# Three real products per frequency slot instead of four in the middle phase of a four-layer graph network

## The reference

```
h = relu(bn(conv1d(xc, conv1_w, 0)))        # 1 tap
h = bn(conv1d(h, conv2_w, 8))               # 17 taps, 128 -> 128 channels, padding 8
x_conv = relu(h + xc)
```

## Time and profile before

| | |
|---|---|
| profiled execution, device time | 1127.47 us |
| its span, first to last instruction | 1125.6 us |
| TensorE busy (matmul) | 1072.3 us, 95% |
| VectorE busy | 826.1 us, 73% |
| ScalarE busy | 715.6 us, 64% |
| GpSimd busy | 595.5 us, 53% |
| mean granted TensorE clock | 0.984 of full |
| DMA | 84.45 MB, mean 75 GB/s |

### The profile page before, as it was taken

One profiled execution on the slowest core, in us unless ns is written; L12 is line 12 of the kernel. 1 busy time (PEld: TensorE's weight loads), 2 busy tenths in 40 slices (PEclk: granted clock), 3 DMA queues, 4 the chain that ended last, 5 costly groups with the idle time before them and its releaser, 6 DMA issues.

```text
span 1125.6 us, 24829 instructions
## 1 busy us (share of the span) xinstructions
PE 1072.3 (95%) x8013; PEld 960.3 (85%) x8013; DVE 826.1 (73%) x2548; ACT 715.6 (64%) x1335; POOL 595.5 (53%) x650
## 2 busy tenths in 40 slices
PE   7899999999999969989999999999999999999884
PEld 6799999999999958968888888888888888888774
DVE  4477777777778732634787888888888888889983
ACT  4444555455555522346777878787878787878765
POOL 1244343434334304633576666676767676766674
PEclk9999999999999969999999999999999999999988
DMA  4112332223332125862111111111111111100001
GB/s 163 55 50 85 95 92 87 87 94 95 95 94 79 55 74 163 254 199 65 58 58 48 57 57 58 57 58 58 58 57 58 58 57 58 39 29 11 20 29 38
DMA packets 64190, 84.45 MB, mean 75 GB/s; under 512 B 6464, under 2 KB 33472, under 8 KB 63808
## 3 DMA queue, kind: packets, MB, share of 16 engines
q1 hardware_dynamic: 64064, 82.86, 23.7%
HBM read 57.14 MB, written 25.69 MB: 74 GB/s over the span
## 4 chain that ended last, share of the span: by engine, by line
PE 90%; DVE 3%; issue 2%; ACT 2%; POOL 1%; DMA 1%; SPq 0%; ACTq 0%; DVEq 0%; POOLq 0%
PE banks L160 19%; PE banks L154 11%; PE banks L155 10%; PE banks L156 10%; PE banks L513 10%; PE banks L771 4%; PE banks L541 3%; PE banks L681 3%; PE banks L606 3%; PE banks L656 3%; PE banks L483 2%; PE banks L635 2%; PE banks L721 2%; PE banks L573 1%; PE banks L609 1%
## 5 line engine op out<-in xcount | busy, mean ns | idle before, releaser
L168 POOL TENSOR_TENSOR rstd<-ve,minus_half 128x4 f32<-128x4 f32 x128 | 131.5, 1027 | 72.0 <-DVE ve L1091 66.0
L168 POOL TENSOR_TENSOR r_rms<-ms,minus_half 128x4 f32<-128x4 f32 x32 | 32.3, 1008 | 224.7 <-DVE ms L1055 224.7
L513 PE MATMUL banks<-w,s 128*128 128x128 f32 x768 | 101.2, 275 | 0.4 <-DVE y L1069 0.4
L513 PEld LDWEIGHTS banks<-w,s 128*128 128x128 f32 x768 | 95.6, 192 | 3.4 <-issue 0.5
L154 PE MATMUL banks<-agg_hi,w_hi 128*128 128x512 f32 x192 | 87.5, 455 | 5.7 <-issue 5.5
L1081 DVE BATCH_NORM_STATS2 stats<-y 128x6 f32<-128x128 f32 x384 | 82.9, 279 | 1.7 <-POOL y L1443 1.5
L155 PE MATMUL banks<-agg_lo,w_hi 128*128 128x512 f32 x192 | 77.1, 402 | 0.0
L156 PE MATMUL banks<-agg_hi,w_lo 128*128 128x512 f32 x192 | 76.8, 400 | 0.0
L160 PE MATMUL banks<-at,x_rows 128*128 128x128 f32 x512 | 69.6, 280 | 3.9 <-DVE agg_lo L1043 3.0
L160 PEld LDWEIGHTS banks<-at,x_rows 128*128 128x128 f32 x512 | 65.9, 196 | 7.0 <-issue 2.3
L771 PE MATMUL banks<-w,z 128*128 128x128 f32 x512 | 68.9, 280 | 3.2 <-DVE t L1285 1.9
(11 more groups left out here) (193 smaller groups left out, 3325.4 us busy)
## 6 DMA issues: line engine op xcount, KB each, us to landing
at<-in_at SPq DMA_DIRECT2D x32, 256.0 KB, 2.9
x_rows<-in_x SPq DMA_DIRECT2D x32, 256.0 KB, 2.9
x_scratch<-x SPq DMA_DIRECT2D x32, 256.0 KB, 3.1
ad<-in_ad SPq DMA_DIRECT2D x32, 256.0 KB, 2.6
x1c<-x_scratch SPq DMA_DIRECT2D x32, 256.0 KB, 2.7
atc<-in_at SPq DMA_DIRECT2D x32, 256.0 KB, 2.9
yh<-yh_scratch SPq DMA_DIRECT2D x64, 128.0 KB, 2.8
out<-out_rows SPq DMA_DIRECT2D x32, 256.0 KB, 2.0
```

What stands on the lines that cost most here:

```text
L168: return nc.gpsimd.tensor_tensor(to[:], base[:], minus_half[:], ALU.pow)
L513: last = pe.matmul(bank[7][:, g, :], s[c][:, g, :], w2[:, c, :], start=(c == 0 and g == 0), stop=(c == H0 - 1), skip_group_check=True)
```

## The change

Each slot's complex product is made from three real products instead of four, with a common half. With transformed taps stored as c + d and c - d (a change of the host's `tap_dft` matrix), the kernel computes m = (a - b)(wd) once, where wd is the difference of the two stored weight halves, halves it, and adds it to each of two products of its own, a times the one half and b times the other. The differences a - b and wd are tiles of four slots (a chunk; 17 chunks), in rings of two. GpSimd makes all weight differences and the data differences of twelve of the chunks; VectorE makes the data differences of chunks 0, 4, 8, 12, 16. The banks 0 and 1 hold the common halves; ScalarE evicts these, times 0.5, a chunk at a time. The banks 2 to 7 hold the pairs; VectorE alone evicts them, adding the common half. The `spectrum` ring has four tiles instead of six. All of the small stores of pairs 0 and 1 now count on one semaphore, so that a wait for either waits for all sixteen. The load of `x1c` and `atc` for group 1 moves from ahead of the stores to behind `load_yh(0)`; `rest_low` makes one quarter instead of two. The first loads of the kernel are in another order. Nothing else of phases one and three is touched, but for tile placement and semaphore counts.

```diff
-        STAGES, STORES = 6, 3
+        STAGES, STORES = 4, 3
-        rest_stored, rest_in = ([sem_of(f"rest_{n}{i}") for i in range(2)] for n in ("stored", "in"))
+        rest_stored, rest_in = sem_of("rest_stored"), [sem_of(f"rest_in{i}") for i in range(2)]
-        spectrum = hn[0:3] + s[0:3]
+        spectrum = hn[0:3] + s[0:1]
+        x_diff, w_diff = s[1:3], [y0, rv]
+        shared = [x1_rows, agg]
+        CHUNKS = SLOTS // G
+        X_BY_DVE = list(range(0, CHUNKS, 4))
+        X_BY_POOL = [c for c in range(CHUNKS) if c not in X_BY_DVE]
         def stored_pair(engine, p):
             if 0 <= p < REST_PAIRS:
-                engine.wait_ge(rest_stored[p], REST_STORES)
+                engine.wait_ge(rest_stored, REST_PAIRS * REST_STORES)
+        def difference(engine, out, of, c):
+            first = 2 * SLOT_ORDER[G * c]
+            return engine.tensor_tensor(out[c % 2][:], of[:, first:first + 2 * G:2, :],
+                                        of[:, first + 1:first + 2 * G:2, :], ALU.subtract)
...
             # SyncE
-            for k in range(2):
-                load_x1(k)
-                load_atc(k)
+            load_x1(0)
+            load_atc(0)
             for p in range(PAIRS):
                 store_slots(p)
...
             load_yh(0)
+            load_x1(1)
+            load_atc(1)
             load_yh(1)
...
             # TensorE
+            def shared_products(c):
+                if c in X_BY_DVE:
+                    pe.wait_ge(sem["x_dve"], X_BY_DVE.index(c) + 1)
+                else:
+                    pe.wait_ge(sem["x_pool"], X_BY_POOL.index(c) + 1)
+                pe.wait_ge(sem["w_diff"], c + 1)
+                if c >= 2:
+                    pe.wait_ge(sem["shared"], c - 1)
+                for i in range(G):
+                    if SLOT_ORDER[G * c + i] > 0:
+                        last = pe.matmul(bank[c % 2][:, i, :], x_diff[c % 2][:, i, :], w_diff[c % 2][:, i, :],
+                                         start=True, stop=True)
+                last.then_inc(sem["shared_ps"], 1)
+            def own_products(p):
+                if p >= 6:
+                    pe.wait_ge(sem["pair_out"], p - 5)
+                for i in range(2):
+                    slot, psum = SLOT_ORDER[2 * p + i], bank[2 + p % 6]
+                    to_even, to_odd = (2 * slot, 2 * slot + 1) if slot == 0 else (2 * slot + 1, 2 * slot)
+                    pe.matmul(psum[:, 2 * i, :], xh[:, 2 * slot, :], wh[:, to_even, :], start=True, stop=True)
+                    last = pe.matmul(psum[:, 2 * i + 1, :], xh[:, 2 * slot + 1, :], wh[:, to_odd, :],
+                                     start=True, stop=True)
+                last.then_inc(sem["pair_ps"], 1)
-            for p in range(PAIRS):
-                if p >= 8:
-                    pe.wait_ge(sem["even_out" if p % 2 == 0 else "odd_out"], (p - 8) // 2 + 1)
-                psum = flat(bank[p % 8])
-                slot_product(psum[:, 0:2 * P], SLOT_ORDER[2 * p])
-                slot_product(psum[:, 2 * P:4 * P], SLOT_ORDER[2 * p + 1]).then_inc(sem["slot_ps"], 1)
+            for c in range(CHUNKS):
+                shared_products(c)
+                own_products(2 * c)
+                own_products(2 * c + 1)
...
             # ScalarE (the set-up block that stood behind pair 6 now stands behind c == 4)
+            def shared_out(c):
+                act.wait_ge(sem["shared_ps"], c + 1)
+                if c >= 2:
+                    act.wait_ge(sem["pair_out"], 2 * (c - 1))
+                first = 1 if SLOT_ORDER[G * c] == 0 else 0
+                nc.scalar.activation(shared[c % 2][:, first:G, :], bank[c % 2][:, first:G, :], ACT.Copy, scale=0.5
+                                     ).then_inc(sem["shared"], 1)
+            for c in range(CHUNKS):
+                shared_out(c)
+                if 7 <= c < 7 + PARTS:
+                    rest_high(c - 7)
...
             # VectorE
+            def pair_out(p):
+                dve.wait_ge(sem["pair_ps"], p + 1)
+                stored_pair(dve, p - STAGES)
+                dve.wait_ge(sem["shared"], p // 2 + 1)
+                both, out = bank[2 + p % 6], spectrum[p % STAGES]
+                own = shared[p // 2 % 2][:, 2 * (p % 2):2 * (p % 2) + 2, :]
...
+                    V.tensor_tensor(out[:].rearrange("p (s h) n -> p s h n", h=2),
+                                    both[:].rearrange("p (s h) n -> p s h n", h=2),
+                                    own.unsqueeze(2).to_broadcast([P, 2, 2, P]), ALU.add).then_inc(sem["pair_out"], 1)
+            x_difference(0)
             for p in range(1, PAIRS, 2):
-                slots_out(p)
+                pair_out(p - 1)
+                pair_out(p)
+                if p // 2 + 2 in X_BY_DVE:
+                    x_difference(p // 2 + 2)
                 if p >= 15 and (p - 15) // 2 < PARTS:
                     rest_low((p - 15) // 2)
...
             # GpSimd
+            w_difference(0)
+            w_difference(1)
+            until(pool, "xh0", GROUPS - 1)
+            until(pool, "xh1", GROUPS - 1)
+            x_difference(1)
+            for c in range(2, CHUNKS):
+                w_difference(c)
+                if c in X_BY_POOL:
+                    x_difference(c)
```

More of the change, by code:

```diff
@@ L201, in graph_layers @@
         wh = sb("wh", [P, HALVES, P])
+        rv = rows("rv")
+        x1_rows, agg = rows("x1_rows"), rows("agg")
         y0 = rows("y0")
@@ L238, in graph_layers @@
         row_inv = sb("row_inv", [P, B])
-        x1c = [rows(f"x1c{i}") for i in range(2)]
-        atc = [rows(f"atc{i}") for i in range(2)]
+        x1c, atc = [rows("x1c0")], [rows("atc0")]
         factor, points_lr = sb("factor", [P, 2, P]), sb("points_lr", [P, 2, P])
@@ L243, in graph_layers @@
         x1_hi, x1_lo = ([rows(f"x1_{n}{i}", F32R) for i in range(2)] for n in ("hi", "lo"))
-        x1c += [rows(f"x1c{i}") for i in range(2, X1C_RING)]
-        atc += [rows(f"atc{i}") for i in range(2, ATC_RING)]
+        x1c += [rows(f"x1c{i}") for i in range(1, X1C_RING)]
+        atc += [rows(f"atc{i}") for i in range(1, ATC_RING)]
         edge, edge_adj, msg = rows("edge"), rows("edge_adj"), rows("msg")
@@ L394, in store_slots @@
             def store_slots(p):
[L395 to L398, removed]
+                sp.wait_ge(sem["pair_out"], p + 1)
                 stored_pair(sp, p - STORES)
@@ L1174, in rest_low, with x_difference @@
+            def x_difference(c):
+                if c >= 2:
+                    dve.wait_ge(sem["shared_ps"], c - 1)
+                difference(V, x_diff, xh, c).then_inc(sem["x_dve"], 1)
             def rest_low(i):
                 dve.wait_ge(sem["rest_hi"], i + 1)
-                for r in (1, 3):
-                    own = slice(G * REST * r, G * REST * (r + 1))
-                    low = rest[own, PART * i:PART * (i + 1), :]
-                    V.tensor_tensor(low, rest_full[i % 2][own], low.bitcast(F32), ALU.subtract
-                                    ).then_inc(sem["rest_lo"], 1)
+                own = slice(G * REST, 2 * G * REST)
+                low = rest[own, PART * i:PART * (i + 1), :]
+                V.tensor_tensor(low, rest_full[i % 2][own], low.bitcast(F32), ALU.subtract
+                                ).then_inc(sem["rest_lo"], 1)
@@ L1381, in _, with w_difference, x_difference @@
                 stage(rms, t - 1)
[L1383 to L1388 removed]
+            def w_difference(c):
+                if c >= 2:
+                    pool.wait_ge(sem["shared_ps"], c - 1)
+                difference(Q, w_diff, wh, c).then_inc(sem["w_diff"], 1)
+            def x_difference(c):
+                if c >= 2:
+                    pool.wait_ge(sem["shared_ps"], c - 1)
+                difference(Q, x_diff, xh, c).then_inc(sem["x_pool"], 1)
+            until(pool, "x1_rows", GROUPS - 1)
+            until(pool, "down", GROUPS - 1)
+            w_difference(0)
+            w_difference(1)
             until(pool, "xh0", GROUPS - 1)
             until(pool, "xh1", GROUPS - 1)
[L1392 to L1399 removed]
+            x_difference(1)
[3 more added lines that the diff above has]
+                    x_difference(c)
             def x1_low(k):
```

114 lines of the change are left out of this document (43 added, 71 removed).

## The result

The changed kernel takes 1132.36 us, the median of four runs (1132.19 to 1134.55). The kernel before, run beside it, takes 1124.16. The ratio is 1.0081 [1.0062, 1.0101], its 95% interval in brackets: **slower**, by 7 to 11 us. The forecast was 1126, in a range from 1120 to 1131.5, so the time lies above the range. The profiled execution took 1132.24 us, of which the span is 1130.3 (before 1127.47 and 1125.6).

A forecast was written before the change was run, and what follows sets the result against it. TensorE was taken as the bound, the DMA queue close behind. 14 us gained against 14.8 lost ended phase two 0.2 us later; with 1.3 at phase three's entry, 1124.6 + 1.5 = 1126 us, range 1120 to 1131.5.

The forecast's parts named there:

- TensorE's work: Phase two: a slot takes three products, 0.67 us instead of 0.88, gaining 14 us over 67 complex slots.
- The start: Start of phase two: TensorE waits for x_difference(0), starting at 430.1 and not 427.8; 2.3 us lost.
- The hole at chunk 4: Phase two, before chunk 4: TensorE waits for a difference queued behind the small stores' landing, until 449.8; 9.2 us lost.
- The clock: Behind the hole at chunk 4: half clock for some 3.5 us of TensorE's work, costing 1.75 us, bounds 0 and 4.9.
- the rival of a long half clock: Phase two, after the hole: 9.8 us of half clock cost 4.9 us and not 1.75; 1129.3 us, chance 0.08.
- VectorE and SyncE's queue behind the stall: Phase two after the hole: first load_rest at 458.6, rounds of 3.1 to 3.3 us, TensorE waits 1.5 us at chunk 16.
- The end of the stores: End of phase two: the last store at about 488.6, the phase ending 0.2 us later than before.
- The landing of stores (rival two): Phase two's four-tile ring: mean landing of about 3.1 us in the loop slows the rounds; 1130 as middle, chance 0.22.
- The queues keep up (rival one): Phase two ends 3.0 us earlier (1121.6), or 3.7 if only the DMA queue binds (1120.9); chance 0.22.
- The entry of phase three: Start of phase three: load_x1(1), now behind load_yh(0), makes codes(1) 0.5 to 2.3 us late; taken as 1.3 us.

The follow-up runs named there:

- e7: Changed kernel with VectorE's differences ahead of the two evictions and the set-up blocks moved forward to its wait for the small stores; 1128.35 us (one run).
- e12: e7 with a ring of six spectrum tiles instead of four, the load of atc for group 0 moved behind the stores; 1129.06 us (one run).
- e13: e8 with the six-tile ring of e12; 1122.62 us, ratio to the kernel before 0.9991; repeated, 1122.73 us, ratio 0.9979.
- e15: e13 with four stores in flight instead of three; 1120.28 us, ratio to the kernel before 0.9953 [0.9936, 0.9970].
- e6: Changed kernel with load_x1(1) issued ahead of load_yh(0); 1133.1 us (one run).
- e3: Changed kernel with GpSimd's differences from chunk 2 on cut to 4 columns instead of 512, so sums use old data; 1129.72 us (one run).
- e8: e7 with pair 1's small stores on ScalarE's queue, the second set-up block behind pair 5, load_x1(1) ahead of load_yh(0); 1126.42 us, ratio to before 1.0023.
- e1: Changed kernel with each of VectorE's data differences ahead of the two evictions; 1131.39 us, ratio to the kernel before 1.0061.
- e2: Changed kernel with the set-up blocks moved forward to where VectorE waits for the small stores; 1133.27 us, ratio to the kernel before 1.0078.
- e9: Changed kernel with each common product issued twice, so four products a slot as before; 1135.61 us (one run).
- e5: Changed kernel with pairs 0 and 1 given their own semaphores again; 1134.05 us, ratio to the kernel before 1.0086.

## Why the prediction was wrong

Step by step, against the steps on record, with times counted from the end of the `xh` copy where the two profiles differ by it:

- **TensorE's work**: right. Three products a slot, 0.22 us each.
- **The start**: right, 2.6 us after the copy (predicted 2.45). But TensorE then ran at half clock until 433.7, where before it was whole; some 2.7 us that the sum did not have.
- **The hole at chunk 4**: right in its mechanism and its end, 21.8 us after the copy (predicted 22.15). The small stores' last issue ended 1.1 us later than reckoned, and the landing took 1.3 us and not 2.7. The hole is 5.9 us and not 9.2, because TensorE came to it 3.0 us later, mostly by the slow start. What sets the phase is the end, so this gave nothing back.
- **The clock**: after the hole half clock until 450.7, 1.6 us lost (1.75 predicted); the rival of a long half clock was false there. But a second stretch, 0.57 over the 8 us from 474 to 482, lies almost wholly behind the wait at chunk 12: 5.8 us of work at half rate, 2.9 lost. Nothing in the prediction had it; the two stretches together (4.5 us lost) come near the 4.9 of the rival, by another way.
- **VectorE and SyncE's queue behind the stall**: this step failed. The set-up blocks were put in at 2.2 and 2.5 us, from rows of the kernel before, and GpSimd's differences were costed "at nothing", because "nothing in the rows comes near". Beside each other the two engines slow each other: 8.6 us for the blocks. The first `load_rest` came 33.9 us after the copy, predicted 31.0. TensorE was to wait once, 1.5 us at chunk 16; it waited 1.55 at chunk 8 and 3.05 at chunk 12. From the end of the hole to TensorE's last product passed 44.6 us, predicted 38.0: of the 6.6 us of excess 3.1 are waits (4.6 against 1.5), 2.8 half clock (4.5 against 1.75), and 0.7 I can't assign. Phase two ended 6.55 us later and not 0.2. The trace of the kernel before had a sign of the contention, in GpSimd's rows and not in VectorE's: beside the second block two of GpSimd's negations, 0.53 us in the median, took 0.88 and 1.42 us, so that these four took 3.25 us and not 2.1.

```profile
452.50 3.25 POOL L1387 TENSOR_SCALAR y<-wh 128x128 f32<-128x128 f32 x4 [0.68 <-PE banks L611]
```

- **The end of the stores**: this step failed too, and by the prediction's own terms. With the first `load_rest` at 458.6, eight rounds of 3.1 to 3.3 us and eight more stores at the 1 us of its first rival, the last store would be issued at 491.4 to 493.0; the forecast has it at 488.6. Measured, the rounds were as forecast, 3.29 us in the mean. But from the last `load_rest` to phase three's first load 12.5 us passed, where the forecast leaves 9.7; the seventeen profiles, before and after, have nowhere less than 11.9. So of the 6.35 us between forecast and measurement 3.0 are the late first `load_rest`, 0.6 the rounds and 2.8 this end.
- **The landing of stores (rival two)**: false by its own sign. The landings took 2.7 us in the median as before, 4.1 at most, and 2.8 in the mean of the stores in the loop (458 to 484 us). The rival needed a mean of about 3.1, which the kernel before had. The ring of four does carry a part: six tiles take 3.7 us off e7 (e12), though not off the changed kernel alone, which wasn't run. The estimated 3.9 by the Trainium skill (DMA: Bandwidth & Descriptors, latency and other measured facts) was reached only near that longest one. The price was near, by another way.
- **The queues keep up (rival one)**: false here, but its gain of 3.0 to 3.7 us in phase two is about what e13 and e15 have (3.0 to 4.4) once the place of the blocks, the order, the small stores and the ring are changed.
- **The entry of phase three**: right, 1.3 us measured and by e6 1.4.

What is shown: the contention. Without it (e3) the first `load_rest` comes 30.6 us after the copy, where 31.0 was predicted, and the rounds stay at 3.27 us. Also shown is that order and place of the blocks together, the small stores (with the second block's place), and the ring each carry a part (e7, e8, e12); their parts don't add up, as e1 and e2 show. What makes the end of the phase long stays open. In the changed kernel the chain of waits runs through TensorE alone there, from 475.66 to 492.13, with the second half clock in it. Ahead of it stands the landing of a store, then the difference of chunk 12 (start, us, what):

```profile
472.47 2.73 DMA yh_scratch<-hn
...
475.24 0.38 DVE s L331
...
475.66 2.08 PE banks L619 x8
...
492.15 0.70 DVE hn L1202
...
492.87 2.15 DMA yh_scratch<-hn
```

But e3 has no half clock there, and its end took 13.3 us.

## What to carry to other kernels

When work moves to VectorE and GpSimd at once, price them by rows in which both are at work, and look at both engines' rows: before, the other engine's operations were short (0.53 us) and it was the one to wait; after, they were long (1.27 us), and a two-column operation of VectorE's of 0.1 us took 0.83. Follow the queue to its last store with the same prices as the rounds before it. Where one in-order engine feeds a chain with a ring on it, one mended wait exposes the next; test mends together as well as alone. And a bound engine's gain (14 us) is worth what the next queue leaves of it: find the queue's own floor first (e9 put the work back for 3.6 us).

## What the runs showed of the hardware

In the changed kernel TensorE's first products behind waits of 3.05 us and more ran at half clock, those behind 1.55 us at full. It is no rule of the wait alone: behind 3.38 us in e5 the eight records took 1.31 us, most of it full clock, and behind the same 3.17 us they took 1.16 us in e12 and 2.07 in e7:

```profile
445.48 1.16 PE L619 MATMUL banks<-y,s 128*128 128x128 f32 x8 [3.17 <-DVE s L331]
444.72 2.07 PE L619 MATMUL banks<-y,s 128*128 128x128 f32 x8 [3.17 <-DVE s L331]
```

Where it came, a wait of 3.05 us cost 6 in all. I had not expected that operations as small as two columns would wait so plainly for GpSimd's (0.83 us for 0.10), nor that the same phase one would end up to 6 us apart between profiles of kernels that share it.
